# Second attention layer of a cross-attention model: work by pairs of head groups, fp32 value products on column halves

## The reference, cut to what matters

```
# second layer, cross-attention: 16 heads H
q_big  = rope(einsum(layernorm(x) @ Wq.T, w_kc_q))          # 192 wide
kv_r   = rope(ctx_512)                                      # 1444 keys, 64 wide
q_r    = einsum('bshq,hqr->bhsr', q_big, W_qr)              # 64 wide
k_r    = einsum('bld,hdr->bhlr', kv_r, W_kr)
attn   = softmax(einsum('bhsr,bhlr->bhsl', q_r, k_r))       # no scale, no mask
ctx_c  = einsum('bhsl,bld->bhsd', attn, kv_r)
x      = x + concat_heads(einsum('bhsd,hkd->bhsk', ctx_c, w_kc_kv)) @ Wo.T
# second layer, feed-forward: int8 activations, ternary weights
h      = silu(qx @ gate) * (qx @ up)                        # 1024 wide
x      = x + bit_linear(rms_norm(h, ln_weight), w_down)
```

## Time and profile before

| | us |
|---|---|
| median of three runs (lowest, highest) | 1182.1 (1175.91, 1184.2) |
| the profiled execution's own time | 1179.18 |
| its span in the profile | 1177.1 |
| PE busy | 1040.8 (88%) |
| DVE busy | 532.0 (45%) |
| ACT busy | 565.0 (48%) |
| POOL busy | 581.0 (49%) |
| mean granted clock of PE, as a share of 2.4 GHz | 0.925 |

### The profile page before, as it was taken

One profiled execution on the slowest core, in us unless ns is written; L12 is line 12 of the kernel. 1 busy time (PEld: TensorE's weight loads), 2 busy tenths in 40 slices (PEclk: granted clock), 3 DMA queues, 4 the chain that ended last, 5 costly groups with the idle time before them and its releaser, 6 DMA issues.

```text
span 1177.1 us, 18220 instructions
## 1 busy us (share of the span) xinstructions
PE 1040.8 (88%) x6680; PEld 837.7 (71%) x6680; DVE 532.0 (45%) x1070; ACT 565.0 (48%) x1205; POOL 581.0 (49%) x785
## 2 busy tenths in 40 slices
PE   5986776997798789999999999999999999999793
PEld 3665664686687478787787788788678778778572
DVE  3234552322234823634834734743653573472513
ACT  2322222221113047647656765765764765677761
POOL 2002220480021058766776767666676664477660
PEclk9867887898898879999999999999999999999996
DMA  9014001568810000000000000000000000000000
GB/s 247 5 58 158 1 1 51 188 204 280 286 39 22 1 14 1 13 2 1 1 18 1 1 18 1 1 18 1 1 18 1 1 1 5 1 1 5 1 4 3
DMA packets 37827, 49.25 MB, mean 42 GB/s; under 512 B 9798, under 2 KB 31352, under 8 KB 37484
## 3 DMA queue, kind: packets, MB, share of 16 engines
q1 hardware_dynamic: 36716, 46.46, 12.6%
q0 software_dynamic: 1024, 1.64, 0.5%
HBM read 42.73 MB, written 5.31 MB: 41 GB/s over the span
## 4 chain that ended last, share of the span: by engine, by line
PE 59%; DVE 14%; issue 8%; ACT 6%; POOL 6%; DMA 5%; SPq 1%; POOLq 0%; DVEq 0%; ACTq 0%
PE ps L1054 8%; PE ps L1011 6%; PE ps L993 5%; DVE nm L1687 5%; PE ps L1038 4%; PE ps L931 4%; PE ps L1068 4%; PE ps L1065 4%; PE ps L1066 3%; POOL pl L627 3%; PE ps L997 3%; PE ps L1096 2%; PE ps L1087 2%; PE ps L742 2%; PE ps L944 2%
## 5 line engine op out<-in xcount | busy, mean ns | idle before, releaser
L627 POOL TENSOR_TENSOR pl<-pt,ph 120x400 fp32r<-120x400 f32 (+1 forms) x384 | 407.5, 1081 | 271.0 <-ACT ph L1456 227.0
L1455 ACT ACTIVATE pt<-ps 120x400 f32<-120x400 f32 (+1 forms) x384 | 193.9, 505 | 151.1 <-PE ps L1054 146.9
L1687 DVE TENSOR_REDUCE nm<-ps 128x1 f32<-128x482 f32 (+1 forms) x312 | 184.1, 650 | 37.2 <-PE ps L1038 36.5
L1456 ACT ACTIVATE ph<-ps 120x400 fp32r<-120x400 f32 (+1 forms) x384 | 192.0, 500 | 0.0
L1054 PE MATMUL ps<-qh,khl 128*120 128x400 f32 (+1 forms) x384 | 149.0, 388 | 8.9 <-ACT ph L1456 5.6
L1054 PE MATMUL ps<-ql,kh 65*120 65x400 f32 (+1 forms) x384 | 134.6, 351 | 0.0
L1068 PE MATMUL ps<-pl,kv 120*65 120x400 f32 (+1 forms) x384 | 133.7, 348 | 0.4 <-POOL pl L627 0.2
L1065 PE MATMUL ps<-ph,kv 120*65 120x400 f32 (+1 forms) x384 | 133.8, 348 | 0.0
L1066 PE MATMUL ps<-ph,kv 120*64 120x400 f32 (+1 forms) x384 | 133.1, 347 | 0.0
L1038 PE MATMUL ps<-khl,qh 128*128 128x482 f32 (+1 forms) x312 | 100.7, 416 | 5.6 <-DVE ql L1679 1.7
L1666 DVE TENSOR_TENSOR xyz<-ps,ropeq 128x400 f32<-128x400 f32 x64 | 33.8, 570 | 157.6 <-PE ps L997 157.6
(11 more groups left out here) (251 smaller groups left out, 1593.2 us busy)
## 6 DMA issues: line engine op xcount, KB each, us to landing
egu<-_L_ffn_gate_up_proj_dram SPq DMA_DIRECT2D x14, 1024.0 KB, 6.0
edn<-in_L_ffn_down_proj_dram SPq DMA_DIRECT2D x14, 512.0 KB, 6.9
craw<-in_ctx_dram SPq DMA_DIRECT2D x8, 360.0 KB
wo_n<-in_L_xattn_Wo_dram SPq DMA_DIRECT2D x1, 2048.0 KB, 10.9
wq_n<-in_L_xattn_Wq_dram SPq DMA_DIRECT2D x1, 2048.0 KB, 9.8
xs_scratch<-zero SPq DMA_DIRECT2D x1, 1792.0 KB, 12.6
xs<-xs_scratch SPq DMA_DIRECT2D x14, 128.0 KB, 6.2
ys_scratch<-ysb SPq DMA_DIRECT2D x14, 128.0 KB, 6.2
```

Of the source, the lines that this page charges most:

```text
L627: nc.gpsimd.tensor_tensor(pl[k % PS_BUF][r, :], pt[k % PT_BUF][r, :], ph[k % PS_BUF][r, :].bitcast(F32), ALU.subtract).then_inc(pl_ready, 1)
L1455: nc.scalar.activation(pt[k % PT_BUF][0:rows, :], ps[0:rows, k % 2, 0:HT], ACT.Exp)
L1456: nc.scalar.activation(ph[k % PS_BUF][0:rows, :], ps[0:rows, k % 2, 0:HT], ACT.Exp).then_inc(ph_ready, 1)
L1687: nc.vector.tensor_reduce(nm3[0:w, i, n:n + 1], ps[0:w, max_bank(b, i) + n, 0:MN], AX.X, ALU.max)\
```

## The change

The unit is now a pair of groups `u` (`NU` = 16 pairs, two per batch), and a unit has `LANE` = 24 slots: for each key tile first the one group, then the other. Query, maxima, sums and context are made per pair. A unit is three stretches of `PHASE` = 8 slots; after each stretch of scores come the value products of its four key tiles.

- Values: no high and low parts. ACT takes one exponential per tile into `pt` (fp32, eight buffers of a pair), and `values` multiplies plain fp32 keys (120 x 64) with the two groups' weights, one to partitions 0 to 63 and one to 64 to 127 of bank 2.
- Sums: POOL adds the pairs of tiles up (`add_weights`, 11 additions of 120 x 800 per pair); `sum_weights` multiplies the total with ones on both halves. ACT copies one row of each half, a DMA lays them on 32 partitions, DVE inverts, and DMAs write the inverse to memory and read it back to all 128 partitions; DVE divides with both operands in SBUF.
- Maxima: 7 tiles of 3 chunks per pair (`MC` = 21), one chunk in each of the slots 1 to 21 for the next pair, in banks 3 and 4 in turn; turned in slot 23. Before the loop stand only those of pair 0.
- Query: `q_big` of the pair after the next in six parts per group, one per slot; `q_latent` in slot 23 for both groups, a product on one half after one on the other.
- Keys are kept in fp32; their low part is made by a new step on DVE (`low_keys`) instead of on POOL.
- Feed-forward: its second half (norm, quantisation, down product) comes one batch later than before, and for batch 6 after the loop.

```diff
-M_SLOT = (14, 18, 22, 24, 26, 28, 30, 32, 34, 36, 37, 39, 40)
+LANE = 2 * KT
+PHASE = 8
+MT = -(-GU // 128)
+MC = 3 * MT
+MAX_FROM, TURN_MAX_AT = 1, 23
+KEEP_AT, INVERT_AT, DIVIDE_AT = 1, 9, 15
+OUT_FROM, RESIDUAL_SLOT, QX_SLOT, X4_SLOT = 17, 21, 23, 19
+GU_SLOT, SILU_SLOT, HIDDEN_SLOT = (40, 41, 44), 42, (43, 46)
+SQ_SLOT, HN_SLOT, H_NORM_SLOT = 1, 4, 3
+QH_SLOT = (7, 17, 20, 23)
+PT_BUF = 8
...
+        def spread_sums(sp, u):
+            sp.wait_ge(sums_kept, u + 1)
...
+            for a in range(2):
+                sp.dma_start(inv[u % 2][RP * a:RP * a + RP, :],
+                             sums[u % 2][CD * a:CD * a + 1, :].rearrange("a (p n) -> a p n", p=RP)).then_inc(sums_spread, 16)
+            sp.wait_ge(sums_inverted, u + 1)
+            sp.dma_start(inv_dram[u % 2:u % 2 + 1, :].rearrange("a (p n) -> (a p) n", p=2 * RP), inv[u % 2][:, :]).then_inc(inv_written, 16)
+            sp.wait_ge(inv_written, 16 * (u + 1))
...
+            for a in range(2):
+                sp.dma_start(spread[u % 2][CD * a:CD * a + CD, :],
+                             inv_dram[u % 2:u % 2 + 1, HT * a:HT * a + HT].to_broadcast([CD, HT])).then_inc(inv_spread, 16)
...
+        def add_weights(pool, j):
+            u, t = j // KT, j % KT
+            pool.wait_ge(p_ready, 2 * j + 2)
+            if t == 0:
+                return
...
+            if t > 1:
+                pool.wait_ge(p_added, (KT - 1) * u + t - 1)
+            before = pt[(j - 1) % PT_BUF] if t == 1 else total
+            nc.gpsimd.tensor_tensor(total[r, :, :], before[r, :, :], pt[j % PT_BUF][r, :, :], ALU.add).then_inc(p_added, 1)
...
+            def q_latent(u):
...
                 for i in range(HG):
                     for j in range(3):
+                        for a in range(2):
+                            last = mm(ps[CD * a:CD * a + CD, 5, S * i:S * i + S], amat[:, 2 * HG * p + HG * a + i, j, :],
+                                      xyz[a][:, j, i, :], start=j == 0, stop=j == 2)
...
+            def scores(k):
+                if k % LANE == 0:
+                    pe.wait_ge(max_row, 32 * (u + 1))
+                    pe.wait_ge(q_lo, u + 1)
                 if k >= 2:
+                    pe.wait_ge(p_ready, k - 1)
+                if k % LANE == PHASE and u:
+                    pe.wait_ge(sums_kept, u)
...
+            def values(j):
+                pe.wait_ge(p_ready, 2 * j + 2)
...
+                for a in range(2):
+                    last = mm(ps[CD * a:CD * a + CD, 2, 0:HT], kv[b % KV_BUF][r, t, :], pt[j % PT_BUF][r, a, :],
+                              start=t == 0, stop=t == KT - 1)
+            def sum_weights(u):
+                pe.wait_ge(p_added, (KT - 1) * (u + 1))
+                pe.wait_ge(p_ready, min(LANE * (u + 1) + PHASE, SLOTS * B))
+                for a in range(2):
+                    last = mm(ps[CD * a:CD * a + CD, 0, 0:HT], ones[0:KP, :], acc[u % 2][:, a, :], start=True, stop=True)
...
+                for s in range(SLOTS):
+                    k, u, at = SLOTS * b + s, PAIRS * b + s // LANE, s % LANE
+                    f, x = at // PHASE, at % PHASE
                     scores(k)
+                    if u + 1 < NU and MAX_FROM <= at < MAX_FROM + MC:
+                        max_chunk(u + 1, at - MAX_FROM)
+                    if u + 2 < NU and f < 2 and 1 <= x <= 6:
+                        q_big(u + 2, f, x - 1)
...
+                    if u + 1 < NU and at == TURN_MAX_AT:
+                        turn_max(u + 1)
+                    if x == PHASE - 1:
+                        if f == 2 and u + 2 < NU:
+                            q_latent(u + 2)
+                        for i in range(4):
+                            if f == 0 and u and i == 3:
+                                sum_weights(u - 1)
+                            values(KT * u + 4 * f + i)
...
+            def divide(u):
...
+                tt(ct[:, HT * p:HT * p + HT], ctu[u % 2][:, :], spread[u % 2][:, :], ALU.mult).then_inc(c_ready, 1)
...
+            hidden_norm(B - 2)
+            for part in range(4):
+                quantise_h(B - 2, part)
+            invert_sums(NU - 1)
+            divide(NU - 1)
```

More of the change, by code:

```diff
@@ L1070, in turn_sums @@
-            def turn_sums(q):
-                pe.wait_ge(sums_kept, q + 1)
-                if q:
-                    pe.wait_ge(c_ready, q)
-                if q % NG == 0 and q // NG + 1 < B:
-                    pe.wait_ge(k_kept, 3 * (q // NG + 2))
-                for i in range(HG):
-                    last = mm(ps[0:S, 7, i:i + 1], sums[q % 2][CD:CD + 1, S * i:S * i + S], ones[CD:CD + 1, 0:1],
-                              start=True, stop=True)
-                last.then_inc(sums_turned, 1)
@@ L1110, in turn_xq, with gate_and_up @@
                 last.then_inc(xq_turned, 1)
-            def gate_and_up(b, half):
-                maxima_read(b, GU_SLOT[half])
+            def gate_and_up(b, part):
+                if part == 0:
+                    pe.wait_ge(xq_kept, b + 1)
+                    pe.wait_ge(x3_ready, b + 1)
+                    pe.wait_ge(rope_done, min(2 * PAIRS * (b + 2) + 4, 2 * NU))
+                    for n in range(2):
+                        for c in range(DC):
+                            last = mm(ps[0:S, 6 + n, :], xqT[:, c, :], wgT[:, c, 512 * n:512 * n + 512],
+                                      start=c == 0, stop=c == DC - 1)
+                    last.then_inc(g_done, 1)
+                    return
+                half = part - 1
                 if half:
@@ L1161, in _ @@
             turn_keys(0, 1)
-            q_big(0, 1)
+            for part in range(6):
+                q_big(0, 1, part)
             turn_ternary(2)
             turn_ternary(3)
-            q_latent(0, 0)
             turn_keys(0, 2)
@@ L1216, in _ @@
[L1216 to L1227 removed]
+                    if b + 2 < B and s == X_SLOT:
+                        turn_x3(b + 2)
@@ L1228, in _ @@
             turn_xq(B - 1)
-            gate_and_up(B - 1, 0)
-            gate_and_up(B - 1, 1)
+            for part in range(3):
+                gate_and_up(B - 1, part)
             pe.wait_ge(h1_part, 2 * B)
@@ L1828, in _ @@
+            for part in range(4):
+                quantise_h(B - 2, part)
+            invert_sums(NU - 1)
+            divide(NU - 1)
+            result(B - 2)
             residual(B - 1)
```

723 lines of the change are left out of this document (350 added, 373 removed).

## The result

The changed kernel takes 1175.6 us in the median of 20 runs (1168.0 to 1180.2), the kernel before 1182.6 in 20 runs beside it: ratio 0.993, 95% interval 0.991 to 0.995. The forecast of 1105 was 71 us too low, and 1175.6 lies outside the range of 1050 to 1152. The profiled execution took 1171.3 (span 1169.6). PE's busy time fell from 1040.8 us to 910.6, so its work did go, by 130 us, and the span kept nearly its length.

A forecast was written before the change was run, and what follows sets the result against it. The prediction took TensorE to bound the loop. Start -9, batches 0 to 6 -69, last batch -10 and tail +10.5 summed to -77 from 1179.2, 1102, plus 3 for the median: 1105 us, range 1050 to 1152.

The forecast's parts named there:

- the paragraph on the DMAs: Sums to 32 lanes, inverse out and back: three landings of 2.8 us, hidden; SP's maxima and stores behind them due later.
- POOL's 55 of 85 us are hidden and eight buffers take the lag: POOL per middle batch: additions 44 us and rotation 11, covered by PE; eight pairs of weight buffers absorb delay.
- The sum without the stop: Whole kernel: middle batch 85.2 us instead of 95.0; start -9, loop -69 and -10, tail +10.5, giving 1105.
- Value pair: Two fp32 value products of 400 columns on the column halves run side by side: 0.74 us (ends 0.65 and 0.91).
- Changes of tiling: PE switching between full-width and half-column products loses 0.15 us each, twelve per batch: +1.8 us.
- q_latent: Query product with two groups on the halves in turn: 5.5 us a batch instead of 8.8, saving 3.3.
- PE work: TensorE's work in a middle batch falls from 88.8 to 75.6 us.
- Waits: PE's waits per middle batch: 5.0 us of the old 6.2 stay, and 4.6 us of new ones come.
- The rival in which the waits vanish: Half of old and new waits go (4.8 us) and values come at 0.65 (2.2): 1055 us; chance 0.25.
- Tail: After the loop, the later feed-forward stands on DVE ahead of the last inversion: +10.5 us, 44 us after the loop.
- DVE held by POOL: Nine DVE instructions a batch each held by a 2 us POOL addition: +6 us a batch, 1150 us; chance 0.2.
- The clock: Rival of no gain: PE waits more, its mean clock falls to 0.89 through the loop: 1180 us; chance 0.03.

The follow-up runs named there:

- e1: The changed kernel with SP loading the keys of batch b + 2 at the start of batch b, ahead of sums and maxima; 1055.4 us, ratio 0.893.
- e4: The changed kernel with SP's order untouched, but POOL rotating the keys in slots 27 to 47 instead of 7 to 47; 1048.9 us, ratio 0.887.
- e11: e10 with the second up product two slots later (46 for 44) and the second half of h in slot 47; 1031.7 us, ratio 0.873.
- e2: e1 with four value tiles of one group multiplied first, then four of the other, so neighbours share a column half; 1114.2 us, ratio 0.942.
- e10: The changed kernel with early key load, late rotation, reordered tail, and silu computed by tanh plus one DVE operation; 1047.8 us, ratio 0.886.
- e9: The changed kernel with early key load, late rotation, reordered tail, and the exponential in place of silu (another function, no table loads); 1028.6 us, ratio 0.867.

## Why the prediction was wrong

**The step that failed** is in the paragraph on the DMAs: "On SP's queue the maxima and stores come behind these and are due later. Hidden". It counts the DMAs that the change moved behind the sums, and leaves out the load of the keys, which the new order of SP's loop puts behind both. Before, it left at 592.1, ahead of the batch that begins at 594.6; after, it waits for maxima that are ready in slot 23, and POOL asks in slot 7. Had the step listed every DMA of SP's loop with the wait in front of it and the slot in which its data is wanted, the 16 slots between 7 and 23, about 25 us, would have stood there. The measured wait is 27.8. e1 and e4 take the cause away from either end and give back 120 and 127 us. With it fell the statement that POOL's 55 of 85 us are hidden and eight buffers take the lag: that holds for POOL's work, but not for 28 us in which it stands. No rival named the load.

**The sum without the stop** was too high as well: 1105 against 1055 of e1. Batches 1 to 6 take 78.0 us there on average and not 85.2, which is 43 us. Batch 0 takes 66.8; the sum had counted it as 9.8 less than before, 75.6. The two errors have opposite signs, so 71 us is their remainder and not the size of either.

**The other terms**, by e1 and e11, where the stop is gone:

- *Value pair*: 0.74 forecast, 0.71 at the pace above, with the way out of the stretch in it. *Changes of tiling*: 0.15 each forecast, some 0.1 measured. Timeline of PE in e1, the chunks ahead of and behind the stretch of values at 724.27 that is shown with e2:

```profile
723.96 0.38 PE L1097 MATMUL ps<-khl,qh 128*128 128x482 f32 x1
...
727.57 0.38 PE L1097 MATMUL ps<-khl,qh 128*128 128x482 f32 x1
727.79 0.34 PE L1117 MATMUL ps<-qh,khl 128*120 128x400 f32 x1
```

The values start 0.31 behind the chunk, and a score 0.22 behind one. The last record of values (0.50 long) starts at 726.68 and the score at 727.10, 0.42 later, where a step inside the stretch is 0.34. So the changes exist and cost about two thirds of their price, but pair and changes together stay below the 0.74 that was put for the pair alone.
- *q_latent*: 2.75 for two groups forecast (half of 5.5), 2.1 measured at full clock. Timeline of PE, kernel after, with the product behind it:

```profile
617.77 2.28 PE L1068 MATMUL ps<-xyz,amat 128*64 128x100 f32 x48
619.88 2.86 PE L1129 MATMUL ps<-pt,kv 120*64 120x400 f32 x16
```

- *PE work*: 75.6 forecast, 71.1 busy in 75 us of e11. The difference is mainly q_big (9.1 instead of 11.0 from start to start, in parts between scores), q_latent and the value pairs with their changes.
- *Waits*: 9.6 forecast, 4.8 left in e1 and 3.9 in e11. The rival in which the waits vanish (1055) has the number of e1, and half of it is also what happened: it priced 4.8 us of waits. Its value pairs of 0.65 did not come, they take 0.71; q_big, q_latent and batch 0 made up for them. That part is luck.
- *Additions on POOL*: 2.0 forecast, 1.90 measured. *Start*: 406 forecast, first score at 407.7. *Tail*: 44 forecast, 45.0 measured from the end of the last value product to the end of the span.
- *DVE held by POOL*: true in its mechanism, and smaller in size. Groups of the kernel after (count, min/median/max ns), and the divide in e11:

```profile
L1790 DVE TENSOR_SCALAR xn<-x_sb,mv,rstd x7: 1947/1948/1965, 541.0 to 1087.0; 100x256 f32<-100x256 f32 x7
L1775 DVE TENSOR_TENSOR ct<-ctu,spread x16: 575/585/1910, 477.7 to 1137.6; 128x400 f32<-128x400 f32 x16
```

```profile
L1776 DVE TENSOR_TENSOR ct<-ctu,spread x16: 575/688/2017, 461.3 to 994.5; 128x400 f32<-128x400 f32 x16
```

`xn` takes 0.41 where no addition runs (after the loop). In the loop it starts together with an addition each time and takes 1.95: it waits for that one and no more, though another stands right behind it. For the divide it matters when it starts. In e11 eight of sixteen start while an addition runs, and every one of them ends 0.43 us after that addition, at 0.80 to 2.02 us. The others take 0.58, also the six in which an addition starts 0.2 us after them. In the changed kernel only three start under an addition, so its median of 0.585 says little about the hold. The rival priced nine held instructions a batch at 2 us each. A middle batch of e11 has `xn` (1.5 us more than alone) and one divide (0.5 more), and 3.9 us of PE's waits for all causes, so the hold was not worth 6. Why `xn` once took 5.15 in the kernel before, under several subtractions, stays open.

**The clock** rival gave 1180 and so has nearly the measured number, and in the loop the clock did fall to the 0.89 that it names (0.89 from 408 to 1058). It is not the reason: the low clock comes after PE has begun to stand, and PE stands through most of it. In the windows of e1 above, PE's busy time is 74.2 us at a clock of 0.96, and with the stop 74.8 at 0.88: 0.6 of 20 us. So the match of the number is luck. The mean over the span is 0.861 with the stop, 0.897 in e1 and 0.925 before.

So the change brings 130 us (e1 against the kernel before on the same chip, 1185.4), and the place of one load on SP took 120 of them.

## What to carry to other kernels

When the loop of a DMA queue is reordered, list for each transfer the wait now in front of it and the slot that wants its data; a transfer whose data depends on nothing in the loop goes ahead of every wait, once its buffer is free. An engine that works in order passes a wait on to everything behind it, so let it ask for prefetched data as late as its reader allows, not as early as the data might be there. And if an engine is idle while the others run, and they stand while it runs, look at what held it first.

## What the hardware showed that was not expected

Two fp32 products of 400 columns on the column halves take 0.71 us when they alternate (e1), and 1.06 with four of each half in a row (e2). In e10 PE stood 2.19 us ahead of one product in a batch of 77 us, and the window behind it had a clock of 0.83; with 0.95 (e9) and 0.43 (e11) it stayed at 1.00. A DVE operation on SBUF that started while an addition of 1.9 us ran on POOL ended only after it: `xn` grew from 0.41 to 1.95, and every such divide of e11 ended 0.43 behind the addition. An addition that started behind the divide did not lengthen it, and in the kernel before the divide with an operand in PSUM took at most 0.58.
